# Loads of finished sums spread over units, and two reciprocals placed after the last maximum, in a three-layer attention block on one core

## What is computed

```python
def _L0_ffn_ref(hidden_states, Wq, bq, Wk, bk, Wv, bv, ..., Wo, bo):
    ...                                   # weights mixed from 4 experts, per batch
    q = moe_proj(Wq, bq).reshape(B, T, H, D)      # B = 2, T = 1024, H = 16, D = 8
    k = moe_proj(Wk, bk).reshape(B, T, H, D)
    v = moe_proj(Wv, bv).reshape(B, T, H, D)
    scores = jnp.einsum('bthd,bshd->bhts', q, k) / np.sqrt(D).astype(np.float32)
    attn = jax.nn.softmax(scores, axis=-1)
    out = jnp.einsum('bhts,bshd->bthd', attn, v).reshape(B, T, C)
    return out @ Wo + bo
x = x + 0.5 * _L0_ffn_ref(_layernorm(x), ...)
x = x + _L0_attn_ref(_layernorm(x), ...)
x = x + 0.5 * _L0_ffn_ref(_layernorm(x), ...)
```

## Time and profile before

| what | value |
|---|---|
| median of 3 runs | 1517.54 us (1509.4 to 1518.91) |
| the profiled execution's own time | 1519.78 us |
| its span, first to last instruction | 1518.1 us |
| mean granted TensorE clock | 0.938 of full |
| busy: PE, DVE, ACT, POOL | 1300.0, 1135.2, 920.7, 334.0 us |
| the 32 units of stage 0, and of stage 1 | about 69 to 424 us, and 1150 to 1500 us |

### The profile page before, as it was taken

One profiled execution on the slowest core, in us unless ns is written; L12 is line 12 of the kernel. 1 busy time (PEld: TensorE's weight loads), 2 busy tenths in 40 slices (PEclk: granted clock), 3 DMA queues, 4 the chain that ended last, 5 costly groups with the idle time before them and its releaser, 6 DMA issues. The chain is left out here.

```text
span 1518.1 us, 28082 instructions
## 1 busy us (share of the span) xinstructions
PE 1300.0 (86%) x8368; PEld 539.0 (36%) x8368; DVE 1135.2 (75%) x1941; ACT 920.7 (61%) x1915; POOL 334.0 (22%) x552
## 2 busy tenths in 40 slices
PE   4699998888866999999988999999958999978895
PEld 2122221122124555555556555555631222212122
DVE  6899997799655677766644666677559999969985
ACT  3288887777735555555533555555425888867774
POOL 4200000110002434343422333343330000001000
PEclk9599999999867999999999999999977999989998
DMA  4511225322102321111110222220051212252211
GB/s 119 167 51 47 57 56 79 69 60 63 29 18 55 75 45 44 43 43 44 44 44 1 52 54 55 53 47 1 22 159 51 55 49 56 59 88 63 60 43 56
DMA packets 58910, 86.49 MB, mean 57 GB/s; under 512 B 22289, under 2 KB 32465, under 8 KB 58833
## 3 DMA queue, kind: packets, MB, share of 16 engines
q1 hardware_dynamic: 58832, 85.53, 24.1%
HBM read 37.79 MB, written 22.54 MB: 40 GB/s over the span
## 5 line engine op out<-in xcount | busy, mean ns | idle before, releaser
L917 DVE TENSOR_REDUCE neg_max<-ps 128x1 f32<-128x1024 f32 x512 | 600.8, 1217 | 76.7 <-PE ps L1158 67.8
L772 ACT ACTIVATE arena<-ps 128x512 f32<-128x512 f32 x1024 | 539.4, 602 | 189.7 <-PE ps L1173 186.9
L1173 PE MATMUL ps<-arena 50*128 50x512 bf16 x1024 | 321.9, 401 | 70.5 <-ACT arena L772 40.3
L993 DVE TENSOR_REDUCE a_neg_max<-ps 128x1 f32<-128x129 f32 (+7 forms) x256 | 193.2, 755 | 168.4 <-PE ps L1275 165.1
L1158 PE MATMUL ps<-arena 48*128 48x512 bf16 x1024 | 276.1, 408 | 26.9 <-DVE neg_max L917 24.8
L1187 PE MATMUL ps<-arena 128*32 128x512 f32 x2048 | 288.4, 637 | 2.8
L579 POOL TENSOR_SCALAR arena<-arena,a_rsum 128x128 f32<-128x128 f32 (+7 forms) x256 | 192.2, 751 | 374.9 <-DVE a_rsum L1001 363.8
L1275 PE MATMUL ps<-arena 128*128 128x512 bf16 (+4 forms) x1344 | 239.7, 305 | 9.5 <-ACT null_out L723 4.8
L1173 PEld LDWEIGHTS ps<-arena 50*128 50x128 bf16 x1024 | 78.5, 95 | 435.1 <-ACT arena L772 362.5
L686 ACT ACTIVATE arena<-ps,a_neg_max 128x129 f32<-128x129 f32 (+7 forms) x256 | 189.7, 742 | 60.6 <-DVE a_neg_max L993 58.5
L696 ACT ACTIVATE arena<-ps 128x128 f32<-128x128 f32 (+1 forms) x192 | 87.1, 454 | 206.4 <-PE ps L1288 205.1
(11 more groups left out here) (120 smaller groups left out, 804.3 us busy)
## 6 DMA issues: line engine op xcount, KB each, us to landing
arena<-stack_dram SPq DMA_DIRECT2D x128, 192.0 KB, 3.3
stack_dram<-arena SPq DMA_DIRECT2D x48, 256.0 KB, 3.8
arena<-arena SPq DMA_DIRECT2D x32, 384.0 KB, 4.4
o_dram<-arena SPq DMA_DIRECT2D x32, 256.0 KB, 2.1
arena<-arena SPq DMA_DIRECT2D x32, 256.0 KB, 5.0
arena<-o_dram SPq DMA_DIRECT2D x30, 256.0 KB, 4.6
arena<-max_dram SPq DMA_DIRECT2D x256, 1.0 KB
arena<-arena SPq DMA_DIRECT2D x32, 128.0 KB, 4.9
```

The lines of the kernel that those rows point to most:

```text
L772: nc.scalar.activation(probs[:, t, :], ps[:, EXP_BANK[t], :], ACT.Exp, scale=F_SCALE).then_inc(probs_ready, 1)
L917: nc.vector.tensor_reduce(neg_max[:, g, t:t + 1], ps[:, bank:bank + 2, :].rearrange("p a b -> p (a b)"), AX, ALU.max, negate=True).then_in ...
L993: nc.vector.tensor_reduce(a_neg_max[:, t:t + 1], ps[:, S_BANK[t % 2]:S_BANK[t % 2] + (n + HALF - 1) // HALF, :].rearrange("p a b -> p (a b ...
L1173: ins = nc.tensor.matmul(ps[:, bank, :], stack[rows, g, 1, kt * P:(kt + 1) * P], stack[rows, g, 0, h * HALF:(h + 1) * HALF], start=True, s ...
```

## The change

Two things move; no operation, transfer or wait is added or dropped.

- `load_o` for pairs 0 to 7 is issued one pair per unit, in units 16 to 23, behind each unit's `max_rows_in`. In units 19, 21 and 23 a load of batch 1 (pairs 8, 9 and 10) stands right behind it. POOL's `sums` moves from unit 21 to unit 25.
- The two `recip_0` of a stage move from behind the maxima of passes 5 and 6 to behind the last transpose, ahead of `normalize_1`.

```diff
--- before.py
+++ after.py
@@ -376,9 +376,8 @@
                             store_o(0, i0 + i, i * 2)
                         if not (last and g == NB - 1):
                             max_rows_in(after[1], after[0])
-                        if isinstance(i, int) and i == HB - 1 and g < 2:
-                            for n in range(g * PAIRS_B // 2, (g + 1) * PAIRS_B // 2):
-                                load_o(n)
+                        if isinstance(i, int) and HB - 1 <= i <= HB:
+                            load_o((i - HB + 1) * NB + g)
                         if isinstance(i, int) and i > HB - 1 and g == 1:
                             load_o(2 * i - 1)
                         if isinstance(i, int) and i >= HB - 1 and g == 3:
@@ -553,7 +552,7 @@
                         if not last or g == 0:
                             prepare((g - 1) % NB, ph * UNITS + ul + g - 1 + NB, ul + g - 1 + NB,
                                     ph == 0 and isinstance(ul, int) and ul + g == 0)
-                        if isinstance(ul, int) and ul == HB * NB and g == 1:
+                        if isinstance(ul, int) and ul == (HB + 1) * NB and g == 1:
                             sums()
                 body(0, False)
                 with pool.Fori(1, HB) as i:
@@ -1090,9 +1089,9 @@
                 for i in range(HB, UNITS // NB):
                     for g in range(NB):
                         maxima(g, i0 + i, False)
-                    if i < HB + 2:
-                        recip_0(ph, i - HB)
                 max_transpose(NB - 1, i0 + UNITS // NB - 1)
+                for g in range(2):
+                    recip_0(ph, g)
                 for g in range(2):
                     normalize_1(ph, g)
                 finish(ph * B, 0)
```

## The result

The changed kernel takes 1478.49 us (median of 4 runs, 1476.77 to 1478.79) against 1518.22 before (1509.40 to 1529.39): a ratio of 0.9732, 95% interval 0.9667 to 0.9797. The profiled execution took 1478.79 us, 41.0 less than the one before. The forecast was 1484.3 with a range of 1476 to 1497.

The account below looks back on a forecast made before the run. PE and DVE, both 92% busy in step, bound the kernel, with stalls from load bursts and reciprocals on top. 20.32 + 15.20 = 35.5 us off 1519.8 gave 1484.3 us, range 1476 to 1497.

Parts of the forecast that it names:

- The bursts: Two bursts of four loads per stage become single loads, removing the backlog that the maxima met: 20.32 us off.
- The cause of the lateness: Transposed maxima on the SP queue land late behind four loads and two stack loads: 5.24 us late, 3.40 of stall.
- Singles cost nothing: One load more per unit than in the steady state does not make the maxima late (1.43 us): nothing.
- The rival of a stall in every unit: Every load ahead of the maxima stalls them, 5.1 us at each of 16 places: 1566 us, chance 0.03.
- Pairs: Two loads together in units 19, 21 and 23: maxima 0.6 to 1.8 us late, 1.0 taken, costing 0 us.
- the 1.84 us that the prediction had to spare: Lateness that the path of the maxima can take before PE stalls: 5.24 - 3.40 = 1.84 us.
- The reciprocals: Two 3.34 us reciprocals per stage leave DVE's stream of maxima: 15.20 us off, with what followed them.
- Their cover at the stage's end: DVE's idle 9.92 and 10.43 us until pair 14 lands takes the 6.68 us added; margins 3.24 and 3.75.
- I leave it as found: Last two units of stage 0 stay slow, 25.3 us against stage 1's 20.0; either end may change by 5.3 us.

Follow-up runs that it names:

- experiment 1: Kernel before with only the two reciprocals of each stage moved behind the last transpose, bursts kept: 1501.92 us against 1515.27, ratio 0.9924.
- experiment 6: Kernel before with its two bursts issued from ScalarE's queue, behind the tenth exponential: 1511.68 us, ratio 0.9981; behind the fourteenth: 1517.30 us, ratio 0.9990.
- experiment 3: Changed kernel with the eight loads of batch 0 going out two per unit in units 16 to 19: 1490.84 us.
- experiment 4: Changed kernel with the eight loads of batch 0 as four pairs in units 16, 18, 20 and 22: 1476.82 us, ratio 0.9744.
- Experiment 2: Changed kernel with the first reciprocal of each stage put back into the stream of maxima, behind those of pass 6: 1496.43 us.
- experiment 8: Changed kernel again, unchanged: 1478.29 us, ratio 0.9749; with one unused reciprocal more per stage behind the maxima of pass 0: 1486.14 us.

## Why the prediction was right

- **The bursts** (20.32 us forecast): confirmed as mechanism and size. The traces give 10.99 + 9.54 = 20.5 us in the units. The timing of experiment 1 against the changed kernel gives 23.4 by the medians and 19.7 from its fastest group, the one with the highest clock.
- **The cause of the lateness**: the prediction spoke of a backlog that the maxima met in SP's queue, and did not ask whether the queue's order or the engines behind it make them late. It is the engines: issued from another queue the same bytes delay them as much (experiment 6).
- **Singles cost nothing**: right, also with a store in the same unit, which the trace of before did not show. The rival of a stall in every unit is excluded by units of 10.3 and 10.5 us throughout.
- **Pairs**: 1.0 us late was taken, between 0.6 and 1.8; the profile shows 0.8 to 1.25 in stage 0, but 1.4 to 2.0 in stage 1. The transfers took 2.3 to 3.4 us where 2 to 3.2 were forecast. Two of the three pairs of stage 1 are beyond the upper bound and beyond the 1.84 us that the prediction had to spare. They cost nothing only because 1.9 to 2.0 us were to spare (experiment 3). So the zero was right with less room than was claimed, and in part by luck. The reason had a gap too: it bounded one pair and assumed that three don't add up. Each pair stands before a unit with one load, which takes most of the lateness back (0.4 to 0.9 left in stage 1); four in a row do add up (experiments 3 and 4).
- **The reciprocals** (15.20 forecast): 7.22 + 8.03 in the units, 13.4 by the timing of the move alone. Their cover at the stage's end: 6.5 of 9.9 and 10.4 us used, 3.9 left, as forecast.
- **The term that was off**: "I leave it as found". The prediction kept one slow stage end, on the ground that shifting the stage might turn either end either way, and sized it at 5.3 us from two rows that don't hold the same work (90 and 94 matmuls). Over the same work it was 7.0 us (28.2 for 21.1), and it went away. The forecast missed the profiled execution by 5.5 us: these 7.0, 0.3 more than forecast in the units, and 1.8 lost elsewhere. The 17 runs without stalls lie within 5.0 us, which leaves hardly any room for an end that is 5.8 us or more too long. Experiment 2, in which a stall was put back, has such ends again; experiment 8 has one run that is as much longer.
- **Still open**: why a stall makes a later stage end slow in some runs and not in others, with many undisturbed units between them. PE's waits at the end itself are no longer than without a stall (4.0 to 5.0 us, for 5.0); the granted clock differs. Nor is it shown that the stall itself is the cause: in the four traces without a stall, the marker's last copy comes 292.0 to 292.7 us behind its fourth in every stage, so a stage without a stall also always ends at the same distance from its start. No run was made that shifts a stage's end without stalling it.

## What to carry to other kernels

When a small transfer on the critical path is late, look at how many bytes were handed to the DMA engines in the microseconds before it, from any queue; spread what is not urgent, and leave room after each larger portion, since a queue whose next loads wait for the late landing carries the lateness on. A few microseconds of an engine's work cost nothing where it waits anyway, but 2 to 4 us each in a stream in which two engines are at 92%: one look at its waits at the end of the stage tells where it fits. Before two stretches are compared, check that they hold the same instructions. And when a kernel's runs scatter, look at the granted clock of the stretches behind its stalls, not only at the stalls' own length.

## What the runs showed of the hardware that was not expected

- Loads from ScalarE's queue delayed an 8 KB transfer of SyncE's queue to 7.7 us from 1.4, as loads in its own queue did; 1 KB transfers that were going out at the same time landed late too (PE waited 2.50 us for them).
- In the stretch of the last two units, in which PE is busy 14.8 of 20.0 us, the granted clock was 1.00 in all eight cases without an earlier stall in the stage. With one it was lower in five of sixteen, part of the stretch being at 1.2 GHz in place of 2.4: 0.60 to 0.70 in four of them, which were 5.8 to 8.4 us longer, and 0.93 in one, 1.7 us longer. The times of kernels with a stall scatter by 7 to 22 us, those without by 5.
- DVE's reciprocal of 128 x 512 f32 (3.3 us) and POOL's product of two tiles of that size (1.27 us) ran at the same time at their usual lengths.
